# The fourth attention's value product from split operands, and a reordered second layer and feed-forward, in an eight-layer fp32 kernel

## The chip, the cores and the metric

The kernel runs on one core of a Trainium2 chip. A core has a matrix engine (PE, with its weight loads shown as PEld), a vector engine (DVE), an activation engine (ACT), a general engine (POOL) and a queue that issues transfers (SP). They run side by side and wait for each other by semaphores. The metric is device time in microseconds, and the median of several runs is what is compared.

## What is computed

The input is `x`, 8 batches of 128 rows of 512 numbers, and a context of the same shape. Four attention-like layers and four feed-forward layers each add their result to `x`. Three of them matter here. The second attention-like layer makes two gains per position from channel maxima and means (a convolution, a norm over the batch, a sigmoid). The third feed-forward is gated:

```
up = xt @ W_up.T
gate = jax.nn.silu(xt @ W_gate.T)
y = gate * up @ W_down.T
```

The fourth attention has 32 query heads over 8 key and value heads, with rotary positions:

```
q = q * cos + _rotate_half(q) * sin
k = k * cos + _rotate_half(k) * sin
k = jnp.repeat(k, GROUPS, axis=1)
v = jnp.repeat(v, GROUPS, axis=1)
scores = jnp.einsum('bhqd,bhkd->bhqk', q, k) / jnp.sqrt(jnp.float32(D))
scores = jnp.where(mask == 0, jnp.float32(-1000000000.0), scores)
attn = jax.nn.softmax(scores, axis=-1)
x = jnp.einsum('bhqk,bhkd->bhqd', attn, v)
return x @ Wo
```

The last line but one is the value product.

## The kernel before

**Split operands.** An fp32 matmul on fp32 tiles is one instruction in the code and two records in the trace. Most products are instead made from a pair: a high part, rounded to the reduced type fp32r (a copy by ACT), and a low part, the rest (a subtraction by POOL or DVE). Three fp32r matmuls, high by high, high by low and low by high, are added up in one bank. The helper is `mm3`, and its three matmuls are L411, L415 and L416 of the trace, whatever they multiply. Weights come as 178 units of 128x512 through a ring: SP loads a unit into `stage`, ACT writes `ring_h` (`hi`, L1210), POOL writes `ring_l` (`lo`, L1030). Every engine runs its own list of instructions, written out by hand in the order of the code, so an instruction that waits holds back all that stands behind it on its engine.

**The fourth attention** takes from 860 to 1372 us of the trace. It runs over 64 blocks, n = 8h + b: head group h (four query heads that share one key head) and batch b. In block n, PE makes the scores of n (L2383, fp32, four matmuls), transposes the probabilities of n - 1 into `bank[2]` (L2394), makes the query projection of n + 5 (`queries3`, twelve fp32r matmuls), the value product of n - 1 (L2407, fp32) and the output projection of n - 2 (twelve fp32r matmuls on `o3h`, `o3l`). The last five blocks have no query projection left.

DVE adds the output of n - 3 to `X` (L1877), masks the scores (L1883, COPY_PREDICATED), takes their bound (L1885), turns the queries of n + 4 by their rotary tables (`rope_queries`, L1861 and L1863), inverts the sums (L1891) and takes the low part of the attention output (L1895). After blocks with b = 1 (h from 1) and b = 5 (h to 6) it also turns half a key tile, the **key step** (`rope_keys`, L1847 and L1849): 14 of them in all. ACT copies the transposed probabilities to `probsT` (L1521), makes the exponentials of n (L1533) and `o3h` (L1543). POOL adds the two halves of the turned queries (L1155), and of the turned keys behind a key step, scales the probabilities of n (L1180), which PE's next transposes wait for, and then makes one or two `ring_l` units in the blocks with b from 2 to 6.

**The gated feed-forward** runs from 636 to 831 us in three groups of hidden tiles f. For each f and each half of the rows PE makes the gate and up products (24 matmuls), ACT and DVE make the hidden tile and its two parts, and after the last f of a group PE makes the down product of the group, which needs all its hidden parts.

**The second layer's gates** run from 292 to 350 us. PE transposes the eight normalised batches (L2126), DVE and ACT make maxima and sums from them, and a convolution (L2140) and two totals (L2144) follow; then ACT makes a gain tile per batch (L1396), which PE transposes (L2152). Key and value pieces of the context (`kv_pe`, 12 matmuls each, evicted by `kv_act`) and the four quarters of the rotary tables (`tables_pe`, L2114, from one-hot tiles that POOL makes at L1087) are set between them as filling.

## Time and profile before

| | us |
|---|---|
| median of 3 runs | 1451.73 (1451.16 to 1452.95) |
| the profiled execution | 1455.56 |
| its span | 1453.4 |

| engine | busy us | share of the span |
|---|---|---|
| PE | 1317.1 | 91% |
| DVE | 957.2 | 66% |
| ACT | 608.1 | 42% |
| POOL | 550.1 | 38% |

The granted clock of PE is 0.96 of full speed over the span. An idle time in the profile stands in front of the instruction that waited, with the engine whose result came last. Matmuls overlap, so the time of one is read from the start of one to the start of the next.

### The profile page before, as it was taken

How to read it: one execution, taken by the hardware profiler on the slowest of the kernel's cores; microseconds unless marked ns; L12 is line 12 of the kernel's file. 1: busy time of each engine (PE TensorE's matmuls, PEld its weight loads, DVE VectorE, ACT ScalarE, POOL GpSimd, SP SyncE). 2: the span in 40 equal slices, each digit the busy share in tenths (PEclk: the TensorE clock that was granted, in tenths of full speed). 3: DMA queues.
4: the chain of work that ended last, by engine and by line, in shares of the span. 5: the costliest groups of instructions: out<-in, count | busy, mean ns of one | idle time of the engine just before them, and what ended most of it. 6: DMA issues, size and time to landing. Idle time of an engine off the chain costs nothing.

```text
span 1453.4 us, 20595 instructions
## 1 busy us (share of the span) xinstructions
PE 1317.1 (91%) x6926; PEld 994.1 (68%) x6926; DVE 957.2 (66%) x2077; ACT 608.1 (42%) x1646; POOL 550.1 (38%) x548
## 2 busy tenths in 40 slices
PE   2887877878999999999999889999999999999797
PEld 1554544666777776687878767777877877777565
DVE  6999956976333688832232666776767777677754
ACT  2787763376213445442121314444333444344341
POOL 5001003553223434152221444464454545544274
PEclk9999886987999999999999999999999999999999
DMA  5211101221221000031110231111121111110001
GB/s 169 59 32 43 30 19 69 80 72 60 73 81 51 1 16 23 1 95 57 44 44 23 66 101 37 31 57 51 37 72 46 59 51 37 51 38 28 1 0 58
DMA packets 53097, 71.41 MB, mean 49 GB/s; under 512 B 5936, under 2 KB 24177, under 8 KB 52995
## 3 DMA queue, kind: packets, MB, share of 16 engines
q1 hardware_dynamic: 52080, 68.89, 15.0%
q10 hardware_dynamic: 914, 1.22, 0.3%
q8 instruction: 57, 0.93, 0.3%
q14 instruction: 46, 0.37, 0.1%
HBM read 55.41 MB, written 10.49 MB: 45 GB/s over the span
## 4 chain that ended last, share of the span: by engine, by line
PE 63%; DVE 17%; issue 6%; POOL 6%; ACT 5%; DMA 2%; SPq 1%; POOLq 0%; DVEq 0%; ACTq 0%
PE bank L411 15%; PE bank L415 14%; PE bank L416 14%; PE bank L2407 3%; DVE topv L1617 2%; PE bank L2287 2%; PE bank L2383 2%; POOL ring_l L1030 2%; PE bank L2269 2%; DVE top L1611 2%; PE bank L2394 1%; DVE bank L1883 1%; PE bank L495 1%; DVE xn L1863 1%; DVE xn L1849 1%
## 5 line engine op out<-in xcount | busy, mean ns | idle before, releaser
L1030 POOL TENSOR_TENSOR ring_l<-stage,ring_h 128x512 fp32r<-128x512 f32 x137 | 181.8, 1345 | 232.7 <-ACT ring_h L1210 232.7
L411 PE MATMUL bank<-xTh_b,ring_h 128*128 128x512 f32 x464 | 190.0, 410 | 4.4 <-issue 3.0
L416 PE MATMUL bank<-xTh_b,ring_l 128*128 128x512 f32 x464 | 184.4, 398 | 0.0
L415 PE MATMUL bank<-xTl_b,ring_h 128*128 128x512 f32 x464 | 184.3, 397 | 0.0
L1155 POOL TENSOR_TENSOR q<-xn 128x512 f32<-128x512 f32 x64 | 82.6, 1291 | 205.4 <-DVE xn L1863 205.4
L411 PE MATMUL bank<-ring_h,o3h 128*128 128x512 f32 x256 | 125.4, 490 | 3.8 <-issue 3.8
L1521 ACT ACTIVATE probsT<-bank 128x512 f32<-128x512 f32 x64 | 38.2, 598 | 203.8 <-PE bank L2394 203.8
L1533 ACT ACTIVATE probs<-bank,nbias 128x128 f32<-128x128 f32 x256 | 90.5, 366 | 51.1 <-DVE nbias L1885 51.1
L411 PEld LDWEIGHTS bank<-xTh_b,ring_h 128*128 128x128 f32 x464 | 88.1, 190 | 24.9 <-issue 6.5
L416 PEld LDWEIGHTS bank<-xTh_b,ring_l 128*128 128x128 f32 x464 | 87.7, 189 | 21.2
L416 PE MATMUL bank<-ring_h,o3l 128*128 128x512 f32 x256 | 101.6, 397 | 0.0
L415 PE MATMUL bank<-ring_l,o3h 128*128 128x512 f32 x256 | 100.9, 394 | 0.0
L415 PEld LDWEIGHTS bank<-xTl_b,ring_h 128*128 128x128 f32 x464 | 88.2, 190 | 18.2
L1863 DVE TENSOR_TENSOR xn<-bank,sinT 64x512 f32<-64x512 f32 x128 | 88.1, 688 | 1.7
L1210 ACT ACTIVATE ring_h<-stage 128x512 fp32r<-128x512 f32 x137 | 81.8, 630 | 13.8 <-DMA stage<-in_units_dram 13.4
L1895 DVE TENSOR_TENSOR o3l<-bank,o3h 128x512 fp32r<-128x512 f32 x64 | 44.3, 692 | 58.1 <-ACT o3h L1543 58.1
L1877 DVE TENSOR_TENSOR X<-X,bank 128x512 f32<-128x512 f32 x64 | 44.0, 687 | 52.1 <-PE bank L416 51.7
L1814 DVE TENSOR_TENSOR hid<-silu,bank 128x512 f32<-128x512 f32 x22 | 15.1, 688 | 93.9 <-PE bank L416 86.4
L1180 POOL TENSOR_TENSOR probs<-probs,rsums 128x512 f32<-128x512 f32 x64 | 66.6, 1041 | 15.5 <-DVE rsums L1891 15.5
L2383 PEld LDWEIGHTS bank<-k,q 128*128 128x128 f32 x512 | 67.7, 193 | 6.9 <-issue 1.7
L2407 PE MATMUL bank<-probsT,v 128*128 128x512 f32 x128 | 67.2, 606 | 4.8 <-ACT probsT L1521 4.8
L1883 DVE COPY_PREDICATED bank<-mask,big 128x512 f32<-128x512 int32 x64 | 59.7, 933 | 13.5 <-PE bank L2383 13.5
(336 smaller groups left out, 3264.4 us busy)
## 6 DMA issues: line engine op xcount, KB each, us to landing
stage<-in_units_dram SPq DMA_DIRECT2D x137, 256.0 KB, 3.0
ring_l<-k SPq DMA_DIRECT2D x64, 64.0 KB, 2.1
raw_k<-kvs SPq DMA_DIRECT2D x16, 256.0 KB, 2.1
kraw<-raw_k SPq DMA_DIRECT2D x16, 256.0 KB, 3.4
v<-raw_v SPq DMA_DIRECT2D x16, 256.0 KB, 2.9
stage<-in_context_dram SPq DMA_DIRECT2D x8, 256.0 KB, 2.9
raw_v<-kvs SPq DMA_DIRECT2D x8, 256.0 KB, 2.0
out_dram<-X SPq DMA_DIRECT2D x8, 256.0 KB, 2.0
```

The lines of the kernel that those rows point to most:

```text
L411: ins = nc.tensor.matmul(out_ap, wh, mh, start=start, stop=False)
L415: nc.tensor.matmul(out_ap, wh, ml, start=False, stop=False)
L416: return nc.tensor.matmul(out_ap, wl, mh, start=False, stop=stop)
L1030: nc.gpsimd.tensor_tensor(ring_l[:, place_of(u), :], stage[:, u % STAGE, :], f32(ring_h[:, place_of(u), :]), ALU.subtract).then_inc(w_lo, 1)
L1155: nc.gpsimd.tensor_tensor(dst, xn[:, (at - 1) % 2, :], xn[:, 2 + (at - 1) % 2, :], ALU.add).then_inc(a3_ad, 1)
L1180: nc.gpsimd.tensor_tensor(pb, pb, rsums[:, n % 4, :].unsqueeze(2).to_broadcast((P, 4, P)), ALU.mult).then_inc(a3_pn, 1)
L1210: nc.scalar.activation(ring_h[:, place_of(u), :], stage[:, u % STAGE, :], ACT.Copy).then_inc(w_hi, 1)
L1533: ins = nc.scalar.activation(probs[:, n % 3, c], bank[n % 2][:, c], ACT.Exp, bias=nbias[:, n % 4, r:r + 1], scale=-1.0, accum_out=psums[:, ...
L1863: ins = nc.vector.tensor_tensor(xn[to, 2 + i % 2, :], src[fro, :], sinT[to, c], ALU.mult)
L1883: link(v, v_chain, nc.vector.copy_predicated(s4, mask3[:, b, :].unsqueeze(1).to_broadcast((P, 4, P)), big[:, :].unsqueeze(1).to_broadcast( ...
L2383: ins = nc.tensor.matmul(bank[n % 2][:, r * P:(r + 1) * P], q3[:, r, c], k3[:, c], start=True, stop=True)
L2407: nc.tensor.matmul(bank[3 + m % 2][:], v3[:, m % 8, :], probsT[:, m % 3, :], start=True, stop=True).then_inc(a3_pv, 1)
```

## The change

Three edits. In the fourth attention the value product becomes an `mm3` of split values and split probabilities. ACT's copy of the transposed probabilities now writes the high part; DVE subtracts it from `bank[2]` right behind the bound of block n (a new instruction per block, between L1885 and L1861 of before) and signals `a3_tl`, for which both the value product and the next transposes now wait. Values are split per half of a head group, by a copy on ACT (`values_high`) and a subtraction on POOL (`values_low`), in the blocks with b = 2 and b = 6. The probabilities have two buffers and not three, and values are loaded again as soon as they are split. In the feed-forward the first half of the next group's first tile is projected before the down product of the group. In the second layer the quarters of the tables and the pieces stand at other places between the transposes, totals and gain tiles. Some semaphores are merged.

```diff
-        put = cTl[:, 0:2, :].rearrange("p a (k c) -> p (a k) c", c=512)
+        pT_h, pT_l = [[cTl[:, i, j * HALF:(j + 1) * HALF] for j in range(2)] for i in range(2)]
+        v3h, v3l = [cTl[:, 2 + i, :].rearrange("p (b e) -> p b e", b=B) for i in range(2)]
...
             def values_load(h, half):
...
-                    sp.wait_ge(a3_pv, B * (h - 1) + 4 * half + 4)
+                    sp.wait_ge(a3_vl, 2 * (h - 1) + half + 1)
...
@@ POOL
-            lo.upto(9)
             one_hot(3)
-            lo.upto(10)
...
+            def values_low(h, half):
+                g.wait_ge(a3_vh, 2 * h + half + 1)
+                c = slice(4 * half, 4 * half + 4)
+                nc.gpsimd.tensor_tensor(v3l[:, c, :], v3[:, c, :], f32(v3h[:, c, :]), ALU.subtract).then_inc(a3_vl, 1)
...
+                if b == 2:
+                    values_low(h, 1)
...
+                if b == 6 and h < 7:
+                    values_low(h + 1, 0)
@@ ACT, second layer
-                if b in (2, 4, 6):
-                    kv_act(a, 6 + b // 2)
-                if b in (3, 5):
-                    hi.upto(9 + b // 5)
+                if b in (4, 6):
+                    kv_act(a, 5 + b // 2)
             kv_act(a, 10)
             tables(0)
-            tables(1)
-            hi.upto(12)
+            hi.upto(10)
...
             gains_by_channel(0)
+            kv_act(a, 11)
+            gains_by_channel(1)
+            tables(1)
             kv_act(a, 12)
+            hi.upto(12)
             for b in range(B):
-                if b + 1 < B:
+                if 1 <= b < B - 1:
                     gains_by_channel(b + 1)
@@ ACT, fourth attention
-                    if m >= 3:
-                        a.wait_ge(a3_pv, m - 2)
-                    nc.scalar.activation(probsT[:, m % 3, :], bank[2][:], ACT.Copy).then_inc(a3_pt, 1)
+                    if m >= 2:
+                        a.wait_ge(a3_pv, m - 1)
+                    nc.scalar.activation(pT_h[m % 2], bank[2][:], ACT.Copy).then_inc(a3_pt, 1)
...
+                if b == 2:
+                    values_high(h, 1)
+                if b == 6 and h < 7:
+                    values_high(h + 1, 0)
@@ DVE, fourth attention
+                if 1 <= n < 65:
+                    m = n - 1
+                    v.wait_ge(a3_pt, m + 1)
+                    nc.vector.tensor_tensor(pT_l[m % 2], bank[2][:], f32(pT_h[m % 2]), ALU.subtract).then_inc(a3_tl, 1)
@@ PE, second layer
-                if b == 1:
+                if b == 3:
+                    kv_pe(t, 7)
+                if b == 5:
                     tables_pe(1)
-                if b in (2, 4, 6):
-                    kv_pe(t, 6 + b // 2)
-                if b == 5:
-                    tables_pe(2)
+                    kv_pe(t, 8)
+            kv_pe(t, 9)
+            tables_pe(2)
             kv_pe(t, 10)
-            tables_pe(3)
...
+            tables_pe(3)
             kv_pe(t, 12)
@@ PE, feed-forward
+            hidden2(0, 0, u)
             for i, group in enumerate(FGROUPS):
                 for f in group:
...
+                    if f > group[0]:
+                        hidden2(f, 0, u)
+                    hidden2(f, 1, u)
                     u += 2
                 last = i == len(FGROUPS) - 1
+                if not last:
+                    hidden2(group[-1] + 1, 0, u + len(group))
@@ PE, fourth attention
-                        t.wait_ge(a3_pt, m)
+                        t.wait_ge(a3_tl, m)
...
-                    t.wait_ge(a3_pt, m + 1)
-                    t.wait_ge(s_v3[m % 8 // 4], 16 * (m // 8 + 1))
+                    t.wait_ge(a3_tl, m + 1)
+                    t.wait_ge(a3_vl, 2 * (m // 8) + m % 8 // 4 + 1)
...
-                    nc.tensor.matmul(bank[3 + m % 2][:], v3[:, m % 8, :], probsT[:, m % 3, :], start=True, stop=True).then_inc(a3_pv, 1)
+                    mm3(bank[3 + m % 2][:], v3h[:, m % 8, :], v3l[:, m % 8, :], pT_h[m % 2], pT_l[m % 2], True, True).then_inc(a3_pv, 1)
```

DVE's list around a key step of the fourth attention, before (`kraw` is the raw key tile, `o3l` the low part of the attention output):

```order
L1883 COPY_PREDICATED bank<-mask,big 128x512
L1885 TENSOR_REDUCE nbias<-bank 128x4
L1861 TENSOR_TENSOR xn<-bank,cosT 128x512
L1863 TENSOR_TENSOR xn<-bank,sinT 64x512 x2
L1891 RECIPROCAL rsums<-psums 128x4
L1895 TENSOR_TENSOR o3l<-bank,o3h 128x512
L1847 SCALAR_TENSOR_TENSOR xn<-kraw,cosT 128x512
L1849 SCALAR_TENSOR_TENSOR xn<-kraw,sinT 64x512 x2
L1877 TENSOR_TENSOR X<-X,bank 128x512
```

and after, on the same engine at the same place (line numbers are those of the changed kernel; `cTl` holds the split probabilities):

```order
L1910 COPY_PREDICATED bank<-mask,big 128x512
L1912 TENSOR_REDUCE nbias<-bank 128x4
L1916 TENSOR_TENSOR cTl<-bank,cTl 128x512
L1888 TENSOR_TENSOR xn<-bank,cosT 128x512
L1890 TENSOR_TENSOR xn<-bank,sinT 64x512 x2
L1923 RECIPROCAL rsums<-psums 128x4
L1927 TENSOR_TENSOR o3l<-bank,o3h 128x512
L1874 SCALAR_TENSOR_TENSOR xn<-kraw,cosT 128x512
L1876 SCALAR_TENSOR_TENSOR xn<-kraw,sinT 64x512 x2
L1904 TENSOR_TENSOR X<-X,bank 128x512
```

The third row is new; the rest keeps its order.

PE's list at the end of the feed-forward's first group, before (banks 0 to 3 take gate and up, banks 4 and 5 the down product):

```order
L411 MATMUL bank3<-xTh_b,ring_h 128x512
L415 MATMUL bank3<-xTl_b,ring_h 128x512
L416 MATMUL bank3<-xTh_b,ring_l 128x512
L411 MATMUL bank4<-ring_h,hid_h 128x512
L415 MATMUL bank4<-ring_l,hid_h 128x512
L416 MATMUL bank4<-ring_h,hid_l 128x512
```

and after:

```order
L413 MATMUL bank3<-xTh_b,ring_h 128x512
L417 MATMUL bank3<-xTl_b,ring_h 128x512
L418 MATMUL bank3<-xTh_b,ring_l 128x512
L413 MATMUL bank0<-xTh_b,ring_h 128x512
L417 MATMUL bank0<-xTl_b,ring_h 128x512
L418 MATMUL bank0<-xTh_b,ring_l 128x512
```

Twenty-four matmuls of the next group (banks 0 and 2) now stand ahead of the down product. The same holds at the end of the second group.

## Rows read from the trace of the kernel before

**Rows 1.** The page: the chain that ended last, shares by engine.

```profile
PE 63%; DVE 17%; issue 6%; POOL 6%; ACT 5%; DMA 2%; SPq 1%; POOLq 0%; DVEq 0%; ACTq 0%
```

**Rows 2.** PE's waits, 905 to 1365: total us, times, longest us.

```profile
PE bank L2407 <- ACT probsT L1521: 4.1, 6, 0.7
...
PE bank L2394 <- POOL probs L1180: 3.0, 8, 0.7
```

**Rows 3.** Timeline, PE, one block: start, duration, us; in brackets idle before.

```profile
1112.44 1.05 PE L2383 MATMUL bank<-k,q 128*128 128x128 f32 x8
...
1116.57 1.02 PE L2407 MATMUL bank<-probsT,v 128*128 128x512 f32 x2
1117.03 0.79 PE L411 MATMUL bank<-ring_h,o3h 128*128 128x512 f32 x1
1117.66 0.39 PE L415 MATMUL bank<-ring_l,o3h 128*128 128x512 f32 x1
...
1120.19 1.05 PE L2383 MATMUL bank<-k,q 128*128 128x128 f32 x8
```

**Rows 4.** Timeline, the same block: POOL's scaling, and PE's next transposes.

```profile
1118.27 1.04 POOL L1180 TENSOR_TENSOR probs<-probs,rsums 128x512 f32<-128x512 f32 x1
...
1121.08 0.60 PE L2394 MATMUL bank<-ident,probs 128*128 128x128 f32 x4
```

**Rows 5.** Timeline around the key step after block 29 (b = 5).

```profile
1093.23 1.28 POOL L1155 TENSOR_TENSOR q<-xn 128x512 f32<-128x512 f32 x1 [3.99 <-DVE xn L1863]
...
1095.06 0.99 DVE L1847 SCALAR_TENSOR_TENSOR xn<-kraw,cosT 128x512 f32<-128x512 f32 x1
1095.46 1.73 POOL L1030 TENSOR_TENSOR ring_l<-stage,ring_h 128x512 fp32r<-128x512 f32 x1
1096.07 2.37 DVE L1849 SCALAR_TENSOR_TENSOR xn<-kraw,sinT 64x512 f32<-64x512 f32 x2
...
1099.08 1.30 DVE L1883 COPY_PREDICATED bank<-mask,big 128x512 f32<-128x512 int32 x1
...
1105.52 0.66 PE L2394 MATMUL bank<-ident,probs 128*128 128x128 f32 x4 [0.33 <-POOL probs L1180]
```

**Rows 6.** Timeline around the key step after block 25 (b = 1).

```profile
1064.58 1.39 DVE L1849 SCALAR_TENSOR_TENSOR xn<-kraw,sinT 64x512 f32<-64x512 f32 x2
...
1072.96 1.27 POOL L1030 TENSOR_TENSOR ring_l<-stage,ring_h 128x512 fp32r<-128x512 f32 x1
...
1074.38 0.47 PE L411 MATMUL bank<-xTh_b,ring_h 128*128 128x512 f32 x1 [0.24 <-POOL ring_l L1030]
```

**Rows 7.** Timeline, block 1: DVE and POOL, POOL busy with `ring_l` until 868.3.

```profile
867.41 1.51 DVE L1883 COPY_PREDICATED bank<-mask,big 128x512 f32<-128x512 int32 x1
...
868.32 1.72 POOL L1155 TENSOR_TENSOR q<-xn 128x512 f32<-128x512 f32 x1
```

**Rows 8.** Timeline, PE, start of the feed-forward's first down product.

```profile
682.13 0.50 PE L411 MATMUL bank<-ring_h,hid_h 128*128 128x512 f32 x1 [1.44 <-DVE hid_l L1805]
```

**Rows 9.** Timeline, PE, the second layer's gates.

```profile
301.41 3.73 PE L2114 MATMUL bank<-hot,probsT 128*128 128x256 f32 x8 [5.46 <-POOL hot L1087]
...
324.48 4.47 PE L2140 MATMUL bank<-rows,bands 128*128 128x32 f32 x24 [2.03 <-DVE rows L1715]
...
344.29 1.11 PE L2152 MATMUL bank<-ident,probs 128*128 128x128 f32 x4 [1.17 <-ACT probs L1396]
```

**Rows 10.** Timeline, PE, the value products of blocks 0 and 59.

```profile
872.46 2.07 PE L2407 MATMUL bank<-probsT,v 128*128 128x512 f32 x2 [0.69 <-ACT probsT L1521]
...
1333.41 1.13 PE L2407 MATMUL bank<-probsT,v 128*128 128x512 f32 x2 [0.69 <-ACT probsT L1521]
```

**Rows 11.** Timeline, PE, two longer waits elsewhere in the kernel.

```profile
280.40 0.47 PE L411 MATMUL bank<-ring_h,lowT_h 128*128 128x512 f32 x1 [1.89 <-DVE lowT_l L667]
...
818.86 0.66 PE L495 MATMUL bank<-ident,xn 128*128 128x128 f32 x4 [2.41 <-DVE xn L462]
```

**Rows 12.** Stretch behind the second: us, PE busy (instructions), granted clock, transfers' share, GB/s.

```profile
819.00:825.00 6.00, 6.00 (x23) 0.72 0.00 1
```

## What the change does to the time: the prediction

> **What bounds the kernel now.** I read the page first: PE is busy 91% of the span and holds 63% of the chain that ended last, DVE 17% of it [rows 1]. So PE's time counts nearly everywhere, and a DVE instruction counts only where PE waits for DVE's work. The list of PE's waits over the fourth attention says where [rows 2]: the value product waits for ACT's copy six times, 4.1 us in all, and the transposes wait for POOL's scaled probabilities eight times, 3.0 us. The timeline of one block shows PE without a gap for 7.75 us [rows 3]. The timelines around the two kinds of key step show the chain behind the small waits: POOL's turn at the probabilities comes late because DVE was late [rows 5, 6]. The feed-forward waits once per group for the last hidden part [rows 8], and in the second layer PE waits for DVE, ACT and POOL [rows 9].
>
> **The value product.** Before, it starts at 1116.57; the first output matmul starts at 1117.03 and its follower at 1117.66, 0.63 later where 0.23 is usual. So it takes 0.46 + 0.40 = 0.86 us [rows 3]. Three fp32r matmuls at 0.23 make 0.70. That is 0.17 us less per block (0.172 with unrounded spacings), and a block of 7.58 us. From block 3 to 58 PE runs without long gaps: 56 x 0.172 = **-9.7 us**. The Trainium skill, "FP8 and Floating Point Precision", section "TensorE Precision Notes", says that true fp32 makes four passes through the array; by that three reduced products would save a quarter of 0.86, 0.22 us a block and 12 us in all. The sum goes by the rows.
>
> **The new subtraction.** No row shows it, but L1895 of the same form (bank less a high part, 128x512) takes 0.69 with 0.61 to 0.66 to the next start. I take 0.65. In an ordinary block it ends before PE asks for it: the query projection (2.9 us) covers copy and subtraction. What it does is push the query turn, POOL's addition and POOL's scaling back by 0.65. The scaling ended at about 1119.3 and the transposes started at 1121.08 [rows 4], 1.8 us of room; 0.65 and PE's own lead of 0.17 leave 0.9. An ordinary block costs nothing. ACT's two and POOL's two splits of values per head group lie in idle time of engines that are 42% and 38% busy, and SP is freed earlier than before.
>
> **The key steps** are where it costs. Behind the step after block 29 DVE is late, and the transposes wait: they could start at 1105.03 (0.89 behind the scores) and start at 1105.52, 0.49 lost [rows 5]. Behind the step after block 25 the scaled probabilities come just in time, but the `ring_l` unit that POOL makes behind them holds the first query matmul until 1074.38, 0.48 late [rows 6]. There are 7 steps of the first kind and 6 of the second with queries still to make (the 14th falls in the last blocks, below). At each, DVE's chain grows by 0.65, starts 0.17 earlier behind the shorter product, and PE arrives 2 x 0.17 earlier: +0.82 each, 13 x 0.82 = +10.7. This is the lower bound of the term.
>
> The upper bound comes from how DVE and POOL get in each other's way. L1849 twice takes 1.39 [rows 6], but 2.37 where a `ring_l` subtraction of POOL runs across it, and COPY_PREDICATED, 0.70 elsewhere, takes 1.30 behind POOL's key addition [rows 5]. In block 1 COPY_PREDICATED stands from 867.41 until POOL's unit ends, then runs, and the POOL addition that starts at 868.32 takes 1.72 for its usual 1.28 [rows 7]. So they exclude each other, and queued instructions take turns. The Trainium skill, "SBUF — State Buffer", section "Who interferes with whom", states such a rule: a DVE instruction with two SBUF inputs and a POOL instruction that reads SBUF block each other fully, one with a single SBUF input does not. By it the new subtraction, with one input in a bank, is itself never held up; 0.65 stands.
>
> Now the places. Before, POOL's query addition (1093.23) and scaling are nearly past when the key step starts at 1095.06 [rows 5]. After, DVE reaches the key step at 1094.89, but POOL's two now start 0.65 later, 1093.88 and 1095.12. Taking turns: L1847 from 1095.05, the scaling to 1096.8, L1849's first half to 1097.4, the `ring_l` unit to 1098.6, the second half to 1099.3. Before it ended at 1098.44, so the collisions put 0.86 on the chain. With the subtraction and PE's earlier arrival that is 0.65 + 0.86 + 0.34 = 1.85 more per step, 13.0 for seven. At the other kind the same turns end at 1066.6 for 1065.97 [rows 6]: 0.65 + 0.63 + 0.34 = 1.62, 9.7 for six. Together **+22.7 us**, and I take this end, since rows 5 and 7 show this very pattern.
>
> **Start and end of the attention.** In block 0 the value product waited for the copy [rows 10]; now it waits for the subtraction too, and that stands ahead of the queries of block 5 on DVE, whose sums' inverse comes 1.5 later, so the second transposes too: 1.4 after PE's gain. In the last five blocks nothing covers copy and subtraction: a product that started 0.69 behind the transposes' end [rows 10] starts about 1.7 later, because the bound of block n stands ahead on DVE. But DVE's other work is the longer path there for three of five; I get +0.7, +0.6, +0.2, +0.1, and +1.4 where the last products wait behind the mask of block 63. **+1.4 and +3.0**; bounds 0 and 7.
>
> **Feed-forward.** The down product starts 1.83 behind the last hidden matmul where 0.23 is usual, and its second matmul 0.11 late [rows 8]: 1.7 lost. At the ends of two of three groups 5.6 us of matmuls now cover that; by the trace their ring units are made more than 10 us before. **-3.4 us.** The third end stays.
>
> **Second layer.** The wait of 5.46 for one-hots, with matmuls at half speed behind it [rows 9], goes: transposes 2 and 3 come at once, DVE runs its batches at 2.63 us each, and by that spacing the sums are ready at 320.5, not 324.15. The convolution starts 3.7 earlier and, with PE not idle before it, may save 1.8 more. But what counts is the third gain transpose, from which PE was dense: 344.29, waiting for ACT [rows 9]. ACT now has between gain tiles 0 and 2 two evictions (1.1), four table copies (2.4) and three ring units (1.8) where one unit and one eviction stood. Adding up from a first gain tile at 334.05 gives 342.7. **-1.6**; bounds -5.7 (all of it, and clock kept) and 0.
>
> **Sum:** -9.7 + 22.7 + 1.4 + 3.0 - 3.4 - 1.6 = +12.4. The profiled execution of 1455.56 would become 1468.0; it stands 3.8 above the median, which becomes 1451.7 + 12.4 = **1464**.
>
> **Rivals.** *No collisions:* the key steps meet POOL as before, the term is 10.7, the sum +0.4: 1452. For it: all collisions hang on some 0.3 us of timing. Against: POOL's two instructions last 2.3 us and DVE must enter between or behind them.
>
> *The clock falls:* a wait of the first kind becomes 0.49 + 1.85 = 2.3 us. Behind waits of 1.89 and 2.41 [rows 11] the granted clock fell to the lower level; it was 0.72 over the 6 us around the second [rows 12], 0.28 x 6 = 1.7 us lost. Behind 1.44 [rows 8] it did not. Seven falls make +11.9: 1476.
>
> *Faster:* the second layer gives back all, -5.7, because ACT gets to gain tile 2 before 341, and the key steps cost only 10.7: 12.4 - 12.0 - 4.1 = -3.7: 1448. It decides at that tile: each us that it comes before 342.7 is a us.
>
> *The change doesn't do what it says:* if DVE waited for ACT's copy in each block, its slack of 0.9 would go first. The copy ended 0.4 before DVE is free for it, so I give this little; 0.1 us a block would be +6: 1470.
>
> **How the numbers follow.** Forecast 0.44 (its own range 1458 to 1470), clock 0.22, no collisions 0.20, faster 0.10, the last 0.04. A measurement here tells about 0.2%, 2.9 us, from no change. Faster is then 0.10; same 0.19, most of "no collisions"; slower 0.71. The range of 1449 to 1475 holds all but the fastest case and the clock cases with more than six falls.
>
> **What would show it.** Blocks of 7.58 us between key steps; transposes waiting 1.9 to 2.2 us for L1180 in every eighth block and the first query matmul some 2 us late four blocks further; L1847 and L1849 together over 4 us in place of 3.4 and 2.4; no wait for `hid_l` at two group ends; the third gain transpose at 342 to 344. It is wrong if the key steps' durations stay, if blocks without one are longer than 7.6, or if the granted clock leaves full speed there.

## The result, and the profile after

| | before | after |
|---|---|---|
| median, us | 1451.45 (4 runs, 1449.91 to 1452.95) | 1472.66 (4 runs, 1469.85 to 1476.14) |
| ratio after / before | | 1.0146, 95% interval 1.0124 to 1.0168 |
| span of the profiled execution, us | 1453.4 | 1474.3 |
| DVE busy, us | 957.2 | 1019.7 |

The changed kernel is 21.2 us slower. The forecast was 1464, which is 12.4 us slower, with a range of 1449 to 1475. The measured time lies in that range, but above the 1458 to 1470 that the prediction gave to its forecast alone, between that and the rival in which the clock falls. The direction and the place (the blocks behind key steps) came out. The size was 8.8 us short. Two signs that the prediction had named came out otherwise: the long waits are not at the transposes, and the granted clock did leave full speed there.

The spans differ by 20.9 us, close to the medians' 21.2, so the two traces can be set side by side stretch by stretch. Each stretch below runs from the start of one PE instruction to the start of another, in us: from the wait for `lowT_l` at 280.40 [rows 11] to the third gain transpose [rows 9]; from the feed-forward's first matmul (635.66 before) to the first scores (859.32); then between the first scores of blocks 0, 3 and 59; then from block 59's to the transposes that wait 2.02 us for `xTl_b` (1374.27 before); and from there to the last matmul.

| stretch | before | after | difference |
|---|---|---|---|
| start to the `lowT_l` wait | 280.40 | 278.81 | -1.6 |
| second layer's gates | 63.89 | 61.47 | -2.4 |
| feed-forward to first scores | 223.66 | 220.59 | -3.1 |
| blocks 0 to 2 | 24.68 | 26.59 | +1.9 |
| blocks 3 to 58 | 440.80 | 460.75 | +20.0 |
| block 59 to the end of the attention | 49.47 | 53.86 | +4.4 |
| last feed-forward | 75.60 | 77.26 | +1.7 |

The stretch between the second and the third line, which the change doesn't touch, took 291.4 us in both. The first and the last line hold no instruction that the change moves or adds. Their differences are the clock's: in eight matmuls of the last feed-forward the spacing was 0.43 us for 0.23. Over all fourteen traces of this study the first stretch lasted from 276.1 to 283.3 us. That is why the experiments below are read by stretch first and by median second.

The page of the changed kernel, the chain by engine, for [rows 1]:

```profile
PE 62%; DVE 21%; issue 6%; POOL 5%; ACT 3%; DMA 2%; SPq 1%; POOLq 0%; DVEq 0%; ACTq 0%
```

DVE went from 17% to 21%. The waits of PE from 905 to 1385 us (total, times, longest), for [rows 2]:

```profile
PE bank L413 <- DVE cTl L1916: 31.8, 20, 2.9
PE bank L413 <- POOL ring_l L1032: 3.8, 6, 0.6
```

L1916 is the new subtraction. The waits for POOL's scaled probabilities are gone; in their place PE waits 20 times at the value product, seven times for 2.04 us, seven times for 0.63 and six times in the last blocks, 13.1 us in all, where no query projection covers the copy and the subtraction. One value product, on PE's timeline (start, duration), for [rows 3]:

```profile
1097.38 0.40 PE L413 MATMUL bank<-cTl 128*128 128x512 f32 x1
...
1097.62 0.40 PE L417 MATMUL bank<-cTl 128*128 128x512 f32 x1
...
1097.85 0.39 PE L418 MATMUL bank<-cTl 128*128 128x512 f32 x1
1098.08 0.39 PE L413 MATMUL bank<-ring_h,o3h 128*128 128x512 f32 x1
```

It takes 0.70 us, as predicted, and blocks without a wait last 7.58 us. The Trainium skill, "FP8 and Floating Point Precision", section "TensorE Precision Notes", gives true fp32 four passes; an estimate from that page was a block of 7.53 us. The trace gives 7.58.

The key step after block 29, all engines, for [rows 5]:

```profile
1099.85 1.22 DVE L1874 SCALAR_TENSOR_TENSOR xn<-kraw,cosT 128x512 f32<-128x512 f32 x1
...
1100.48 1.49 POOL L1188 TENSOR_TENSOR probs<-probs,rsums 128x512 f32<-128x512 f32 x1
...
1101.08 3.13 DVE L1876 SCALAR_TENSOR_TENSOR xn<-kraw,sinT 64x512 f32<-64x512 f32 x2
1101.93 1.73 POOL L1032 TENSOR_TENSOR ring_l<-stage,ring_h 128x512 fp32r<-128x512 f32 x1
...
1104.29 1.29 POOL L1155 TENSOR_TENSOR k<-xn 128x512 f32<-128x512 f32 x1 [0.63 <-DVE xn L1876]
1104.85 1.29 DVE L1910 COPY_PREDICATED bank<-mask,big 128x512 f32<-128x512 int32 x1
...
1106.78 0.68 DVE L1916 TENSOR_TENSOR cTl<-bank,cTl 128x512 fp32r<-128x512 f32 x1
...
1107.52 0.50 PE L413 MATMUL bank<-cTl 128*128 128x512 f32 x1 [2.04 <-DVE cTl L1916]
```

The key step takes 4.35 us for 3.36 before: POOL's scaling and its ring unit now run right across it. DVE comes to the mask of block 30 late, the mask meets POOL's key addition and takes 1.29 us, and the subtraction, which stands behind the mask, comes so late that PE waits 2.04 us for it. The block lasts 10.25 us in place of 7.58. After the key step behind block 25, for [rows 6]:

```profile
1068.03 2.13 DVE L1876 SCALAR_TENSOR_TENSOR xn<-kraw,sinT 64x512 f32<-64x512 f32 x2
...
1073.48 0.50 PE L413 MATMUL bank<-cTl 128*128 128x512 f32 x1 [0.62 <-DVE cTl L1916]
...
1079.17 0.47 PE L413 MATMUL bank<-xTh_b,ring_h 128*128 128x512 f32 x1 [0.63 <-POOL ring_l L1032]
```

There are two waits of 0.6 us, in two blocks. Of the seven waits of 2.04, three (blocks 6, 14 and 54) were followed by a fall of the clock: those blocks lasted 11.8 us, the other four 10.2. The next two rows are the stretch behind block 6's wait and the one from the end of block 30's, which was as long (length in us, busy times, then the granted clock, which is the third number from the end):

```profile
910.00:913.00 3.00, 3.00 (x10) 2.38 (x9) 1.41 (x3) 1.12 (x2) 2.38 (x3) 0.67 0.00 0
...
1107.00:1110.00 3.00, 2.48 (x11) 2.05 (x12) 2.94 (x6) 2.93 (x11) 0.46 (x1) 1.00 0.00 0
```

The two other edits show in these rows, for [rows 9] and [rows 8]: the third gain transpose, and the down products of the feed-forward's first and third groups. The first down product no longer waits.

```profile
340.28 1.12 PE L2185 MATMUL bank<-ident,probs 128*128 128x128 f32 x4 [5.35 <-ACT probs L1405]
...
682.17 0.40 PE L413 MATMUL bank<-ring_h,hid_h 128*128 128x512 f32 x1
...
800.96 0.50 PE L413 MATMUL bank<-ring_h,hid_h 128*128 128x512 f32 x1 [1.44 <-DVE hid_l L1832]
```

### The profile page after: what moved, and what is told of

It is laid out like the page before. It is cut to its first block, busy times and chain, and to the rows that moved or that the text cites. A ratio compares the mean times of both kernels' runs of the same rounds, so it can differ in the third digit from the quotient of the medians.

```text
span 1474.3 us, 20833 instructions
## 1 busy us (share of the span) xinstructions
PE 1312.0 (89%) x6990; PEld 1004.9 (68%) x6990; DVE 1019.7 (69%) x2141; ACT 615.5 (42%) x1662; POOL 579.9 (39%) x564
## 4 chain that ended last, share of the span: by engine, by line
PE 62%; DVE 21%; issue 6%; POOL 5%; ACT 3%; DMA 2%; SPq 1%; POOLq 0%; DVEq 0%; ACTq 0%
PE bank L413 16%; PE bank L418 15%; PE bank L417 15%; DVE topv L1644 2%; PE bank L2425 2%; DVE bank L1910 2%; PE bank L2320 2%; DVE xn L1876 2%; DVE top L1638 2%; PE bank L2302 2%; POOL ring_l L1032 2%; DVE xn L1890 1%; DVE cTl L1916 1%; PE bank L497 1%; DVE nbias L1671 1%
## 5 line engine op out<-in xcount | busy, mean ns | idle before, releaser
L1544 ACT ACTIVATE cTl<-bank 128x512 fp32r<-128x512 f32 x64 | 38.3, 598 | 210.0 <-PE bank L2436 210.0
L1556 ACT ACTIVATE probs<-bank,nbias 128x128 f32<-128x128 f32 x256 | 90.5, 366 | 77.7 <-DVE nbias L1912 77.7
L413 PE MATMUL bank<-ring_h,o3h 128*128 128x512 f32 x256 | 103.9, 406 | 0.7 <-issue 0.7
L1910 DVE COPY_PREDICATED bank<-mask,big 128x512 f32<-128x512 int32 x64 | 76.9, 1202 | 13.9 <-PE bank L2425 13.9
L1188 POOL TENSOR_TENSOR probs<-probs,rsums 128x512 f32<-128x512 f32 x64 | 72.9, 1138 | 16.5 <-DVE rsums L1923 16.5
L2425 PE MATMUL bank<-k,q 128*128 128x128 f32 x512 | 68.2, 276 | 0.0
L1310 ACT ACTIVATE probs<-bank,nbias 128x128 f32<-128x128 f32 x192 | 54.8, 372 | 18.1 <-DVE nbias L1671 17.8
```

Of the source, the lines that this page charges most:

```text
L413: ins = nc.tensor.matmul(out_ap, wh, mh, start=start, stop=False)
L1188: nc.gpsimd.tensor_tensor(pb, pb, rsums[:, n % 4, :].unsqueeze(2).to_broadcast((P, 4, P)), ALU.mult).then_inc(a3_pn, 1)
L1310: ins = nc.scalar.activation(probs[:, n % 3, c], bank[n % 2][:, c], ACT.Identity, scale=-1.0, bias=nbias[:, n % 4, h:h + 1])
L1556: ins = nc.scalar.activation(probs[:, n % 3, c], bank[n % 2][:, c], ACT.Exp, bias=nbias[:, n % 4, r:r + 1], scale=-1.0, accum_out=psums[:, ...
L1910: link(v, v_chain, nc.vector.copy_predicated(s4, mask3[:, b, :].unsqueeze(1).to_broadcast((P, 4, P)), big[:, :].unsqueeze(1).to_broadcast( ...
L2425: ins = nc.tensor.matmul(bank[n % 2][:, r * P:(r + 1) * P], q3[:, r, c], k3[:, c], start=True, stop=True)
```

## The experiments

Each run has its own ratio to runs of the kernel before on the same chip. "Stretch 3 to 59" is the 440.80 us of before. What it would be without any wait is 56 x 7.58 = 424.5 us with the split product and 56 x 7.755 = 434.3 with fp32.

**The value product back in fp32, the other two edits kept.**

```diff
-                    mm3(bank[3 + m % 2][:], v3h[:, m % 8, :], v3l[:, m % 8, :], pT_h[m % 2], pT_l[m % 2], True, True).then_inc(a3_pv, 1)
+                    nc.tensor.matmul(bank[3 + m % 2][:], v3[:, m % 8, :], probsT[:, m % 3, :], start=True, stop=True).then_inc(a3_pv, 1)
```

> The changed kernel with the value product back in fp32 (no split of values or probabilities, no new subtraction); the reordered second layer and the feed-forward hoist stay. Theory (all of the loss is in the fourth attention, and the other two edits keep what the trace of the changed kernel shows: 4.0 us at the gates and 3.0 us at two feed-forward group ends): 1451.5 - 7.0 = 1444.5 us, ratio 0.995, and the attention's blocks as before the change, 7.75 us with 0.5 more behind each key step. Rival (the gains of the other two edits are given back by falls of the granted clock elsewhere): 1448 to 1452.

Measured: 1450.47 us, ratio 0.9983 (0.9965 to 1.0000); stretch 3 to 59 is 440.80, the number of before to the hundredth; gates 62.00 (-1.9), feed-forward 220.57 (-3.1). The time missed the theory's 1444.5 and lies in the rival's 1448 to 1452. So the whole loss comes from the split product, and the other two edits give 5.0 us in their own stretches, but by the ratio only some 2.5 (0 to 5) arrive in the total. In this trace the last feed-forward lasted 77.17 us (a clock fall, +1.6) and the last blocks 0.9 more. Whether such falls are commoner in this kernel than in the one before, as the rival has it, can't be told from one trace of each and is not shown.

**The split product alone, in the kernel before.** Its edit is the first of the change, with the merged semaphores:

```diff
-                    nc.tensor.matmul(bank[3 + m % 2][:], v3[:, m % 8, :], probsT[:, m % 3, :], start=True, stop=True).then_inc(a3_pv, 1)
+                    mm3(bank[3 + m % 2][:], v3h[:, m % 8, :], v3l[:, m % 8, :], pT_h[m % 2], pT_l[m % 2], True, True).then_inc(a3_pv, 1)
```

> The kernel before with the split value product alone (and the merged semaphores it needs). Theory: 1472.7 + 7.0 = 1479.7 us, ratio 1.019; blocks of 7.58 us, the block behind each key step with b = 5 lasting 10.2 us, or 11.8 where the granted clock falls. Rival (the split alone is cheaper and the edits disturb each other through the ring units' timing): 1470 to 1475.

Measured: 1482.29 us, ratio 1.0202 (1.0161 to 1.0244), stretch 3 to 59 459.25, with two clock falls. The theory said 1479.7 and holds, from the other side: without the two other edits the kernel is 29 us slower than before, with them 21. In this trace the unchanged stretch between the gates and the feed-forward was also 5.5 us longer, which is again the clock.

**The subtraction ahead of the mask, behind key steps.**

```diff
+                if 1 <= n < 65 and b in (2, 6):
+                    probs_low(n - 1)
                 if n < 64:
                     v.wait_ge(a3_s, n + 1)
```

> The changed kernel with DVE's new subtraction ahead of the score mask, in the blocks with b = 2 and b = 6 only, which are those behind the key steps. Theory A (what costs is the subtraction's place behind the mask, so that the value product waits 2.04 us for it): that wait falls to 0.3, the block is 1.7 us shorter seven times and 0.6 six times, and the clock stays at full speed: 1472.7 - 12 - 4 - 4 = about 1453 us. Theory B (what costs is how late DVE is behind a key step, whoever waits for it): the bound of block n comes no earlier, so the next transposes wait about 1.7 us for POOL's scaled probabilities instead, and the time is 1470 to 1474.

Measured: 1462.64 us, ratio 1.0066 (1.0046 to 1.0086), stretch 3 to 59 448.15. Neither theory holds alone. PE's waits in the stretch:

```profile
PE bank L2441 <- POOL probs L1188: 7.5, 7, 1.1
PE bank L413 <- POOL ring_l L1032: 4.0, 6, 0.7
```

The wait did move to the transposes of the next block, as in theory B and as the prediction had it, but it is 1.1 us there and not 1.7. The first kind of key step (b = 5) costs 2.0 us over two blocks (8.31 + 8.87, for 2 x 7.58) in place of 2.7. So most of the cost is DVE's lateness whoever waits for it. The new place took 0.65 off each time. That has two parts which this run doesn't separate: the value product no longer waits behind the mask, and the mask, which now comes later, no longer meets POOL's key addition (0.69 us for 1.29). There was also no clock fall in the stretch.

**The key step in two blocks (cosine and first sine part at the end of b = 0 or 4, the rest at the end of b = 1 or 5).**

```diff
+                if b in (4, 5) and h < 7:
+                    rope_keys(h + 1, 0, ((0, 1), (2,))[b - 4])
```

> The changed kernel with each key step spread over two blocks: its first two instructions (the cosine part and the first sine half) at the end of the block with b = 0 or 4, the second sine half at the end of b = 1 or 5; nothing else moves. Theory B (DVE's queue, which has about 1.2 us of idle time in an ordinary block, is overfilled by 2.4 to 4.4 us of key step in one block): the waits of 2.04 and 0.63 us shrink to under 0.3, no block lasts over 8.0 us, and the time is about 1442 us (1438 to 1447). Rival (DVE and POOL stop each other wherever the key instructions stand, so that half the lateness stays): 1455 us.

Measured: 1459.84 us, ratio 1.0047 (1.0029 to 1.0065), stretch 3 to 59 447.68. The theory said 1442, 18 us less; the rival's 1455 is nearer. DVE and POOL at the end of block 28, and the wait this leads to:

```profile
1085.94 1.44 DVE L1875 SCALAR_TENSOR_TENSOR xn<-kraw,cosT 128x512 f32<-128x512 f32 x1 [0.70 <-POOL q L1155]
...
1086.78 1.75 POOL L1032 TENSOR_TENSOR ring_l<-stage,ring_h 128x512 fp32r<-128x512 f32 x1
...
1087.39 1.69 DVE L1878 SCALAR_TENSOR_TENSOR xn<-kraw,sinT 64x512 f32<-64x512 f32 x1
...
1091.77 0.50 PE L413 MATMUL bank<-cTl 128*128 128x512 f32 x1 [1.43 <-DVE cTl L1919]
```

Two instructions that take 0.69 each when alone took 3.1 together, since POOL was at work again; and the first had to wait 0.70 for its tile. POOL makes its query addition and its scaling at the end of every block, so the end of another block is no better place.

**One ring unit out of the key step's way.**

```diff
-                    lo.upto(min(U_L3X + 8 * h + (9, 11, 12, 13, 14)[b - 2], N_UNITS))
+                    lo.upto(min(U_L3X + 8 * h + (9, 11, 13, 13, 14)[b - 2], N_UNITS))
```

> The changed kernel with one ring unit per head group made in the block with b = 4 in place of b = 5 (its copy on ACT and its subtraction on POOL), so that POOL's subtraction no longer runs across the key step behind b = 5. Theory (DVE and POOL exclude each other, and of the key step's 4.35 us about 1.3 is POOL's unit): the three key instructions take about 3.0 us, the wait for the split probabilities in the next block falls from 2.04 to about 0.8 us, that block from 10.25 to about 9.0. Rival (the key step's length is its own or is set by other traffic): 4.3 us and 2.04 us stay.

Measured, in one run: 1460.12 us, stretch 3 to 59 450.05, the block behind the key step 9.19 us, no clock fall in the stretch. This is the theory's side, short of its full size (it had 0.8 and 9.0). The key step after block 29:

```profile
1092.43 1.22 DVE L1874 SCALAR_TENSOR_TENSOR xn<-kraw,cosT 128x512 f32<-128x512 f32 x1
1093.05 1.49 POOL L1188 TENSOR_TENSOR probs<-probs,rsums 128x512 f32<-128x512 f32 x1
...
1093.66 2.13 DVE L1876 SCALAR_TENSOR_TENSOR xn<-kraw,sinT 64x512 f32<-64x512 f32 x2
...
1099.11 0.50 PE L413 MATMUL bank<-cTl 128*128 128x512 f32 x1 [1.05 <-DVE cTl L1916]
```

With POOL's unit away L1876 goes from 3.13 to 2.13, and PE's wait from 2.04 to 1.05: here a microsecond less on the key step is a microsecond less of waiting on PE.

**Key steps on 32 of 512 columns** (the rest of those keys is left out).

```diff
+                w = 32 if h else HALF
+                c = slice(half * HALF, half * HALF + w)
-                nc.vector.scalar_tensor_tensor(xn[:, i % 2, :], kraw[:, half, :], SCALE3, cosT[:, c], ALU.mult, ALU.mult)
+                nc.vector.scalar_tensor_tensor(xn[:, i % 2, 0:w], kraw[:, half, 0:w], SCALE3, cosT[:, c], ALU.mult, ALU.mult)
```

> The changed kernel with every key step of the attention's blocks made on 32 of its 512 columns (the rest of those keys isn't turned: part of the computation is left out). Theory (the whole loss in the middle of the attention is DVE's lateness behind key steps, and the new subtraction costs nothing in any other place): every block from 3 to 58 lasts 7.58 to 7.7 us, the first scores of block 3 to those of block 59 take 425 to 428 us, for 440.8 before and 460.75 after the change; about 1438 us in all. Rival (part of the loss is the split itself: its buffers, its values' splits, the clock): 432 us or more for that stretch.

Measured, in one run: 1455.45 us, stretch 3 to 59 436.70, where the theory said 425 to 428 and the rival 432 or more. So something is left, as the rival said, and 8.7 of the 12.2 us over the floor of 424.5 lie in the blocks with b = 6, which still lasted 8.8 us. The reason stands on DVE's and POOL's timeline:

```profile
1092.19 0.72 DVE L1876 SCALAR_TENSOR_TENSOR xn<-kraw,cosT 128x32 f32<-128x32 f32 x1
...
1092.82 1.04 POOL L1188 TENSOR_TENSOR probs<-probs,rsums 128x512 f32<-128x512 f32 x1
1092.93 2.23 DVE L1878 SCALAR_TENSOR_TENSOR xn<-kraw,sinT 64x32 f32<-64x32 f32 x2
...
1093.82 1.28 POOL L1032 TENSOR_TENSOR ring_l<-stage,ring_h 128x512 fp32r<-128x512 f32 x1
```

The key step takes 2.95 us with a sixteenth of its columns. Nearly all of this is waiting: each of its three instructions ends only when an instruction of POOL has ended, and one that found POOL idle, in the key steps behind b = 1, took 0.19 us. The Trainium skill, "SBUF — State Buffer", section "Who interferes with whom", states such an exclusion for a DVE instruction with two SBUF inputs, and none for one with a single SBUF input. The trace agrees on both: the new subtraction, with one input in a bank, never lasted over 0.69 us.

**Each key step cut in three, one part per block, where POOL has nothing to do**, between the subtraction (or the bound) and the query turn, in a tile of its own; first with the split product, then with fp32.

```diff
+                if n < 64 and 0 < h and b < 3:
+                    rope_keys_part(h, 1, b)
+                if n < 64 and h < 7 and 4 <= b < 7:
+                    rope_keys_part(h + 1, 0, b - 4)
                 if n < 64:
                     if n + 4 < 64:
                         rope_queries(n + 4)
```

> The changed kernel with each key step cut into its three instructions, one each in three blocks in a row (b = 0, 1, 2 and 4, 5, 6), between the new subtraction and the query turn, where POOL has nothing to do; they write to a tile of their own. Theory (each block has about 0.9 us of slack behind the subtraction, and a part is 0.6 to 0.7 us long if POOL doesn't stop it): no wait over 0.3 us in the middle of the attention, block 3 to 59 in 426 us, 1439 us in all (1435 to 1443), ratio 0.992. Rival (the slack is smaller than a part, and each of 40 blocks loses 0.3 us): 1450 us.

> As the run before it (key steps in three blocks each), but with the fp32 value product and no split. Theory: the 0.5 us behind each key step goes, blocks of 7.75 us throughout, block 3 to 59 in 434.4 us, 1444 us in all; so the split product is worth 9.7 us less about 2.5 at the start and the end, some 6 us, once the key steps are out of its way. Rival: the split's gain is eaten in other places, and both kernels come out within 2 us.

Measured: 1462.06 us, ratio 1.0067 (1.0051 to 1.0084), and 1456.42 us, ratio 1.0026 (1.0013 to 1.0040); stretch 3 to 59 448.94 and 448.19. Both expectations missed. The key step in b = 4 to 6 did what it should: the block behind it went from 10.25 to 8.05 with the split product, and with fp32 all blocks there lasted 7.75. But the blocks with b = 3 lasted 9.5 and 9.7: POOL's key addition, left at the end of b = 1 in POOL's list, now waited for the third part in b = 2 and held back the ring units behind it.

**POOL's key addition a block later** (and, in the second kernel, the last six value products in fp32).

```diff
-                if b == 1 and h:
-                    key_sum(h, 1)
+                if b == 2 and h:
+                    key_sum(h, 1)
                 if n + 4 < 64:
                     query_sum(n + 4)
```

> As the run with the fp32 value product and the key steps in three blocks each, but POOL's addition of a key half now stands at the start of the block in which its last part is made (behind the ring units of b = 2, ahead of the query addition), not at the end of the block before, where it held back POOL's ring units. Theory: the 0.2 us at b = 2 and 1.95 us at b = 3 that the run before showed go, block 3 to 59 in 435 us for 448.2, 1444 us in all (1441 to 1448), ratio 0.994. Rival (the part of the key step on DVE is what delays POOL there): 1450 us and more.

> The same two moves (key steps in three blocks each, POOL's key addition a block later) in the changed kernel with its split value product, and the last six value products (batches 2 to 7 of the last head group) in fp32 again, without the new subtraction, since no query projection covers it there. Theory: block 3 to 59 in 432 us for 448.9 in the run with the same key steps and the late addition of POOL, and the last blocks 2.5 us shorter than with the split: 1462.1 - 17 - 2.5 = 1442.5 us (1439 to 1448), ratio 0.993. Rival (with 0.65 us more on DVE in each block the parts of the key step don't fit): 1450 us.

Measured: 1453.28 us, ratio 1.0010 (0.9993 to 1.0027), and 1454.95 us, ratio 1.0014 (0.9995 to 1.0032); stretch 3 to 59 445.83 and 445.78. Both expectations missed again: the blocks with b = 3 stayed at 9.7 with fp32 and 9.8 with the split product, two of these at 11.3 because the clock fell (3.1 us of the 445.78). POOL at b = 2 in the fp32 kernel, and the wait in the block with b = 3:

```profile
1064.96 2.92 POOL L1031 TENSOR_TENSOR ring_l<-stage,ring_h 128x512 fp32r<-128x512 f32 x2 [2.77 <-ACT ring_h L1211]
...
1067.84 1.29 POOL L1155 TENSOR_TENSOR k<-kxt 128x512 f32<-128x512 f32 x1
1069.09 1.28 POOL L1155 TENSOR_TENSOR q<-xn 128x512 f32<-128x512 f32 x1
...
1073.19 0.47 PE L415 MATMUL bank<-xTh_b,ring_h 128*128 128x512 f32 x1 [1.11 <-POOL ring_l L1031]
```

At b = 2 POOL has two ring units that ACT gives it late, and they fill the block up to the query addition. The key addition between them makes everything behind it 1.3 us later. There is no room on POOL at b = 2, but there is at b = 1.

**The first kind of key half a block earlier (parts at b = 7, 0 and 1, the addition at the start of b = 1).**

```diff
-                if n < 64 and 0 < h and b < 3:
-                    rope_keys_part(h, 1, b)
+                if 7 <= n < 64 and b in (7, 0, 1) and n < 58:
+                    rope_keys_part((n + 1) // B, 1, (n + 1) % B)
```

> The kernel with the fp32 value product and key steps in three blocks each, with the first kind of key half one block earlier (its parts in the blocks with b = 7, 0 and 1, and POOL's addition of it at the start of b = 1, where POOL has no ring unit to make). Theory (the 1.94 us that the block with b = 3 still lost came from POOL, whose key addition stood behind two ring units that waited for ACT at b = 2): block 3 to 59 in 434.5 us for 445.8, 1442.5 us in all (1440 to 1446), ratio 0.994. Rival (the ring unit of b = 3 is late for another reason, ACT or the transfer): 1450 to 1453.

> The same shift of the first kind of key half in the kernel with the split value product (fp32 for the last six products). Theory: block 3 to 59 in 429 us (7.58 us each, with 0.5 to 0.9 us lost in a few), 5 us less than with the fp32 product; 1439 us in all (1436 to 1444), ratio 0.991. Rival (with the additional 0.65 us on DVE per block the parts and the splits of values still push POOL's ring units): 1446 to 1452, and the fp32 product is the better one.

Measured: with fp32 1443.63 us, ratio 0.9934 (0.9910 to 0.9959), as expected; with the split product 1445.35 us, ratio 0.9945 (0.9929 to 0.9961), for an expected 1439. Both beat the kernel before and the changed one; the two ratios can't be told apart. With fp32 PE waits for no other engine in blocks 3 to 58; the stretch is 434.19 us, 56 blocks of 7.755. POOL at b = 2, now without the key addition:

```profile
1055.54 2.53 POOL L1031 TENSOR_TENSOR ring_l<-stage,ring_h 128x512 fp32r<-128x512 f32 x2 [2.74 <-ACT ring_h L1211]
...
1058.02 1.31 POOL L1155 TENSOR_TENSOR q<-xn 128x512 f32<-128x512 f32 x1
```

With the split product the stretch is 436.10 us, not the 429 expected, and 11.6 over its own floor of 424.5. Blocks with b = 5 last 8.15 and those with b = 7 last 8.26. The list of PE's waits in the stretch has one kind only:

```profile
PE bank L2453 <- POOL probs L1196: 4.0, 14, 0.4
```

These are the transposes of just those blocks, which wait for POOL's scaling; the two kinds of block lose 8.7 of the 11.6 us. (The waits are booked short: that of 0.37 below moves the transposes 0.53 later than in a block without one.) What comes before the wait of block 29 (b = 5), and then, from 1101.05 on, the wait of block 31 (b = 7):

```profile
1077.09 2.54 POOL L1034 TENSOR_TENSOR ring_l<-stage,ring_h 128x512 fp32r<-128x512 f32 x2
...
1078.38 1.80 DVE L1927 COPY_PREDICATED bank<-mask,big 128x512 f32<-128x512 int32 x1 [0.20 <-PE bank L2442]
...
1080.83 0.68 DVE L1933 TENSOR_TENSOR cTl<-bank,cTl 128x512 fp32r<-128x512 f32 x1
1081.43 0.68 DVE L1877 SCALAR_TENSOR_TENSOR probsT<-kraw,cosT 128x512 f32<-128x512 f32 x1
...
1085.45 1.04 POOL L1196 TENSOR_TENSOR probs<-probs,rsums 128x512 f32<-128x512 f32 x1
...
1086.54 0.66 PE L2453 MATMUL bank<-ident,probs 128*128 128x128 f32 x4 [0.37 <-POOL probs L1196]
...
1101.05 1.04 POOL L1196 TENSOR_TENSOR probs<-probs,rsums 128x512 f32<-128x512 f32 x1
...
1102.15 0.66 PE L2453 MATMUL bank<-ident,probs 128*128 128x128 f32 x4 [0.23 <-POOL probs L1196]
...
1103.76 1.29 POOL L1180 TENSOR_TENSOR cTl<-v,cTl 128x512 fp32r<-128x512 f32 x1
1104.09 1.52 DVE L1877 SCALAR_TENSOR_TENSOR probsT<-kraw,cosT 128x512 f32<-128x512 f32 x1
```

In block 28 DVE has the mask, held to 1.80 us beside POOL's ring units, then the new subtraction and then a part of the key step, all ahead of the query turn. POOL's scaling starts 8.16 us behind the block's first scores, where with fp32 it starts 6.84 behind them. Of these 1.32 us the mask makes 0.72 (it takes 1.08 with fp32) and the subtraction 0.60. In block 30 it is 7.76 for 6.77, with 0.40 from the mask and 0.60 from the subtraction. So the subtraction uses up the room that the part of the key step needs, and the mask meets POOL's ring units for longer. The splitting of values on POOL (L1180) also meets a part of the key step and stretches it from 0.69 to 1.52, but behind the wait, and the next block, with b = 0, loses only 0.08 us. Even with the key steps out of the way the split product is no gain: it takes 9.7 us off PE in the stretch, and the waits behind DVE and POOL give them back.

## Why the prediction came out as it did

- **Value product, -9.7.** This was right: it takes 0.70 us, and blocks last 7.58.
- **The new subtraction costs nothing in an ordinary block.** This was right: those blocks last 7.57 to 7.59 us.
- **Key steps of the first kind, 1.85 more each, +13.0.** The lateness was well worked out: the key step got 0.99 us longer where 0.86 was computed, and takes over 4 us. The station, that is the instruction of PE that waits, was wrong. The prediction looked at the subtraction in an ordinary block and at the transposes behind a key step, and not at the subtraction behind a key step. There it stands behind the mask of a late DVE, and the value product wants it a block earlier than the transposes want POOL's result. A block of 10.25 for 7.58, less the 0.54 of before, makes +2.13 each and +14.9. This is the step that failed, worth 1.9 us by itself. The run with the subtraction ahead of the mask shows the predicted station, with a wait of 1.1 us and 1.5 more per step than before, for the 1.85 computed.
- **The clock, 0 in the sum.** A rival had seven falls of 1.7 us at waits of about 2.3. There were seven waits of 2.04 and three falls of 1.6, +4.7. The forecast took none and the rival all, and "the granted clock leaves full speed there" was one of the prediction's own signs of being wrong. It is the largest single term of the miss. That three waits brought a fall and not none or seven is luck, as far as these traces show.
- **Key steps of the second kind, 1.62 more each, +9.7.** They cost 1.96 us over three blocks, for 0.48 before: +1.48 each, +8.9. The size is near, but the first query matmul is not some 2 us late; it waits 0.63, and the value product of the block before waits 0.62 for the subtraction. The key step took 2.90 for 2.4, which fits the sum; the sign "over 4" was true for the first kind only. The seventh, behind block 57, was put into the last blocks and costs another 0.9 in the stretch, and block 4 0.3.
- **Start +1.4, last five blocks +3.0.** Measured were +1.9 and +4.4. In the other traces with the split product the start took 24.9 to 26.3 us, for 26.6 here and 24.7 before, so part of the 1.9 is this execution's clock (0.69 in block 2, for 0.88 to 0.90 in the three of them that were looked at). The last blocks have waits of 2.42, 2.40, 1.68, 2.21, 2.93 and 1.47 and two clock falls, where before had one. The sum is inside the bounds of 0 and 7.
- **Feed-forward, -3.4.** Measured was -3.1, at the two group ends named; the third still waits 1.44.
- **Second layer, -1.6.** Measured was -2.4, and -1.9 in the run with fp32. The gain transpose came at 340.28 and not at 342 to 344, 1.6 of it because this execution was ahead before the gates; with fp32 it came at 342.67.

In sum +12.4 was predicted, and +20.9 was measured between the traces. The difference of 8.5 is 4.7 (clock in the blocks), 1.9 (first kind), 1.2 (blocks 58 and 4), 1.4 (last blocks) and 0.5 (start), less 0.8 (second kind) and 0.8 (gates), 0.3 of the feed-forward that did not come, and 0.1 in stretches that the change doesn't touch.

Of the rivals, "no collisions" is out by the 4.35 us of the key step. The claim that POOL's and ACT's splits of values cost nothing held: in the changed kernel the blocks behind those with b = 6 last 7.58, and where such a split met a part of the key step the next block lost 0.08.

## What to carry to other kernels

An instruction that is moved from a busy engine to one with slack has to be priced where that engine is latest, at the first consumer in its own block, and not in the ordinary block. Where DVE and POOL exclude each other, an instruction can cost what POOL has in flight rather than its own columns (0.98 and 1.24 us for 0.19 here). So the cure is its place in the block, and cutting it into parts helped only once each part, and POOL's step that follows it, stood where the other engine had room. Before an engine is relieved, look at what makes the waits that are there already: moving the key steps took blocks 3 to 58 from 440.8 to 434.2 us with the old product, and the new product added nothing to that.

## What the hardware showed that was not expected

- Instructions of DVE on 32 columns took 0.72, 0.98 and 1.24 us beside POOL, and 0.19 where POOL was idle. The profile books this waiting as DVE's busy time, so a busy share can hold much that is not work.
- Seven waits of PE of 2.04 us in the same surroundings: the granted clock fell to the lower level behind three and stayed at the upper one behind four. Shorter waits can do it too: in the split kernel with POOL's key addition a block later, waits of 0.66 and 1.11 us a little apart were followed by a fall in two of six like blocks. And the wait of 1.89 us for `lowT_l` [rows 11], the same in all fourteen traces, was followed by a fall in ten of them (0.76 over 7 us, the kernel before among them) and by none in four (1.00, the changed kernel among them). What decides was not settled.
- Before the first changed instruction the executions differ by up to 7 us (276.1 to 283.3 us to the same wait). The best of the kernels here gains 9.6 us by its ratio.
